# Expert token finding in rounds of two slot tiles, with one product per tile, and gathers spread over the scatter-adds

## What is computed

```python
probs = jax.nn.softmax(logits, axis=-1)
flat_probs = probs.transpose(2, 0, 1).reshape(En, T)
scores, tok_idx = jax.lax.top_k(flat_probs, cap)
xf = x.reshape(T, Dn)
toks = xf[tok_idx]
h = jax.nn.gelu(jnp.einsum('ecd,edh->ech', toks, w1) + b1[:, None, :])
y = jnp.einsum('ech,ehd->ecd', h, w2) + b2[:, None, :]
y = y * scores[..., None]
routed = jnp.zeros_like(xf).at[tok_idx.reshape(-1)].add(y.reshape(-1, Dn))
shared = jax.nn.gelu(xf @ sw1 + sb1) @ sw2 + sb2
out = (routed + shared).reshape(Bn, Sn, Dn)
```

## Time and profile before

| | us |
|---|---|
| median of three runs | 3782.42 (3778.78 to 3782.71) |
| the profiled execution's own time | 3778.83 |
| its span | 3777.0 |
| granted TensorE clock, mean over the span | 0.964 |
| tail phase, first product to the end of the span | 3120 to 3777 |

### The profile page before, as it was taken

One profiled execution on the slowest core, in us unless ns is written; L12 is line 12 of the kernel. 1 busy time (PEld: TensorE's weight loads), 2 busy tenths in 40 slices (PEclk: granted clock), 3 DMA queues, 4 the chain that ended last, 5 costly groups with the idle time before them and its releaser, 6 DMA issues. The chain is left out here.

```text
span 3777.0 us, 89362 instructions
## 1 busy us (share of the span) xinstructions
PE 3433.2 (91%) x30012; PEld 2631.4 (70%) x30012; DVE 2437.3 (65%) x6227; ACT 1999.1 (53%) x3884; POOL 2280.0 (60%) x2633
## 2 busy tenths in 40 slices
PE   7999999989999989999999999997997879879883
PEld 4577877777787767878777777774445666667763
DVE  2267776667777667777566777667986888653110
ACT  0156666656666656666665666674653433213331
POOL 0356663766665486666286666366985653464876
PEclk9999999999999999999999999998998999989887
DMA  6867664056766036666225667501111223232433
GB/s 221 259 117 130 129 128 81 19 100 125 130 128 128 8 75 129 129 126 133 46 40 108 129 128 130 95 2 36 33 28 38 64 60 45 54 85 44 71 59 31
DMA packets 456055, 342.06 MB, mean 91 GB/s; under 512 B 70659, under 2 KB 440171, under 8 KB 455595
## 3 DMA queue, kind: packets, MB, share of 16 engines
q1 hardware_dynamic: 404419, 275.69, 37.2%
q10 hardware_dynamic: 24224, 46.44, 3.7%
q0 software_dynamic: 27136, 16.42, 3.2%
HBM read 227.69 MB, written 109.29 MB: 89 GB/s over the span
## 5 line engine op out<-in xcount | busy, mean ns | idle before, releaser
L762 DVE TENSOR_REDUCE a_neg_max<-a_S 99x4 f32<-99x788 f32 x1024 | 1003.5, 980 | 473.6 <-PE a_S L337 470.3
L549 ACT ACTIVATE a_shared<-a_St 99x792 f32<-99x792 f32 (+1 forms) x1024 | 850.3, 830 | 631.7 <-PE a_St L354 620.1
L337 PE MATMUL a_S<-a_k_st,a_q_st 96*99 96x197 bf16 x4096 | 538.5, 254 | 40.1 <-DVE a_neg_max L762 40.1
L354 PE MATMUL a_St<-a_q_st,a_k_st 99*99 99x198 bf16 (+1 forms) x4096 | 529.0, 251 | 43.6 <-DMA a_q_st<-a_max_rows 27.0
L337 PEld LDWEIGHTS a_S<-a_k_st,a_q_st 96*99 96x99 bf16 x4096 | 389.7, 126 | 255.9 <-DVE a_neg_max L762 220.1
L373 PE MATMUL a_O<-a_shared,a_v_aug 99*32 99x198 f32 (+1 forms) x8192 | 466.8, 341 | 0.4
L354 PEld LDWEIGHTS a_St<-a_q_st,a_k_st 99*99 99x99 bf16 (+1 forms) x4096 | 391.1, 126 | 74.3 <-DMA a_q_st<-a_max_rows 34.4
L373 PEld LDWEIGHTS a_O<-a_shared,a_v_aug 99*32 99x32 f32 (+1 forms) x8192 | 247.7, 110 | 85.4 <-issue 2.6
L689 POOL CAST a_parts<-a_q_k 128x792 bf16<-128x792 f32 x128 | 107.8, 842 | 316.4 <-issue 270.1
L1822 POOL DMA_INDIRECT out<-h,token x128 | 209.6, 1638 | 103.9 <-DVE h L1872 47.4
L489 PEld LDWEIGHTS a_O<-a_w,a_shared 128*99 128x99 f32 x2048 | 242.7, 166 | 40.8 <-issue 23.2
(11 more groups left out here) (265 smaller groups left out, 7496.8 us busy)
## 6 DMA issues: line engine op xcount, KB each, us to landing
a_shared<-in_x ACTq DMA_DIRECT2D x64, 594.0 KB, 4.9
spill_q<-a_parts SPq DMA_DIRECT2D x384, 99.0 KB
spill_k<-a_parts SPq DMA_DIRECT2D x384, 99.0 KB
a_k_st<-spill_k SPq DMA_DIRECT2D x128, 297.0 KB
a_q_st<-spill_q SPq DMA_DIRECT2D x128, 297.0 KB
a_k_st<-spill_k SPq DMA_DIRECT2D x128, 198.0 KB
a_q_st<-spill_q SPq DMA_DIRECT2D x128, 198.0 KB
a_k_st<-spill_k SPq DMA_DIRECT2D x128, 99.0 KB
```

Of the source, the lines that this page charges most:

```text
L337: mm = nc.tensor.matmul(S[0:TC, j // 2, j % 2 * TB:j % 2 * TB + NTOK], q_st[p % 4][0:SPLIT, head, b * TB + c * TC:b * TB + (c + 1) * TC], ...
L354: mm = nc.tensor.matmul(St[0:keys, j // 2, j % 2 * TB:(j % 2 + 1) * TB], k_st[p][:, head, first:first + keys], q_st[p][:, head, b * TB:(b ...
L549: nc.scalar.activation(probs[0:keys, u % 4, :].rearrange("p (x t) -> p x t", x=2), St[0:keys, :, 0:2 * TB], ACT.Exp).then_inc(s["probs"], 1)
L762: nc.vector.tensor_reduce(out.rearrange("p (x y) -> p x y", x=2), S[0:TC, :, 0:2 * TB].rearrange("p x (y t) -> p x y t", y=2)[:, :, :, 0:N ...
```

## The change

- The two numbers per block lose their low part where it can go: the first token's number is stored as the number of the block (an integer up to 63) and multiplied by BLK on DVE. Three extra columns are left (RUN = BLK + 3): the first slot's high part, the block's number, the first slot's low part.
- A tile is found by one product of 232 columns. High and low part of the first slot are subtracted one after the other on DVE instead of being summed in PSUM.
- A round is two tiles and fills one bank; even rounds use C, odd ones X. `find` waits for the tokens of the round before the last.
- The four rounds of a turn stand, on PE, after half of `up(n + 1)`, after all of it, after half of `down(n)`, and after all of it. On DVE: rounds 0 and 1, one-hot, round 2, the sum, round 3.
- POOL gathers 13 experts ahead, and the other three in pairs of DMAs after the first twelve scatters.

```diff
-RUN = BLK + 4
+RUN = BLK + 3
-AHEAD = 12
+AHEAD = 13
...
                 def find(e, r, turned):
+                    n_r = 4 * e + r
                     if r == 0:
                         wait(pe, s["t_start"], 1)
                         wait(pe, s["hot"], 2 * (e + 1))
-                    wait(pe, s["token"], 4 * e + 2 * r)
+                    wait(pe, s["token"], n_r - 1)
                     wait(pe, s["copied"], turned)
-                    for k in range(4):
-                        at = r * WL + XCOLS[k]
-                        bank, to = (C, X)[k // 2], k % 2 * 256
-                        one = hot[e % 2][:, at:at + XL]
-                        nc.tensor.matmul(bank[0:XL, to:to + BLK], one, run64[:, e, 0:BLK], start=True, stop=True)
-                        for part in range(2):
-                            mm = nc.tensor.matmul(bank[0:XL, to + BLK:to + BLK + 2], one,
-                                                  run64[:, e, BLK + 2 * part:BLK + 2 * part + 2],
-                                                  start=(part == 0), stop=(part == 1))
+                    for t in range(2):
+                        at = r // 2 * WL + XCOLS[r % 2 * 2 + t]
+                        mm = nc.tensor.matmul((C, X)[r % 2][0:XL, t * 256:t * 256 + RUN], hot[e % 2][:, at:at + XL],
+                                              run64[:, e, :], start=True, stop=True)
                     mm.then_inc(s["found"], 1)
...
                     if n + 1 < PAIRS + UNITS:
-                        up(n + 1)
+                        up(n + 1, range(2))
+                    if e is not None:
+                        find(e, 0, turned)
+                        found += 1
+                    if n + 1 < PAIRS + UNITS:
+                        up(n + 1, range(2, 4))
...
                     if e is not None:
-                        find(e, 0, turned)
-                        found += 2
+                        find(e, 1, turned)
+                        found += 1
...
+                    if e is not None:
+                        find(e, 2, turned)
+                        found += 1
                     down(n, range(2, 4))
                     if e is not None:
-                        find(e, 1, turned)
-                        found += 2
+                        find(e, 3, turned)
+                        found += 1
...
                 for e in range(E):
                     scatter(e)
-                    if AHEAD + e // 2 < E:
-                        gather(AHEAD + e // 2, (0, 1) if e % 2 == 0 else (2, 3))
+                    if AHEAD + e // 4 < E:
+                        gather(AHEAD + e // 4, (e % 4,))
...
                 def tokens(e, r):
-                    n_r = 2 * e + r
-                    two = [bank[:].rearrange("p (t n) -> p t n", n=256) for bank in (C, X)]
+                    n_r, p = 4 * e + r, r % 2
+                    bank = (C, X)[p][0:XL, :].rearrange("p (t n) -> p t n", n=256)
+                    at = local[:, 2 * p:2 * p + 2]
                     dve.wait_ge(s["found"], n_r + 1)
-                    for k in range(2):
-                        nc.vector.tensor_tensor(local[:, 2 * k:2 * k + 2], slot[:, 4 * r + 2 * k:4 * r + 2 * k + 2],
-                                                two[k][0:XL, :, BLK], ALU.subtract).then_inc(s["local"], 1)
-                    for k in range(4):
-                        dve.wait_ge(s["local"], 2 * n_r + 1 + k // 2)
-                        nc.vector.tensor_scalar(junk[:, k, :], two[k // 2][0:XL, k % 2, 0:BLK], local[:, k:k + 1], None,
+                    nc.vector.tensor_tensor(at, slot[:, 2 * r:2 * r + 2], bank[:, :, BLK],
+                                            ALU.subtract).then_inc(s["local"], 1)
+                    dve.wait_ge(s["local"], 2 * n_r + 1)
+                    nc.vector.tensor_tensor(at, at, bank[:, :, BLK + 2], ALU.subtract).then_inc(s["local"], 1)
+                    dve.wait_ge(s["local"], 2 * n_r + 2)
+                    for t in range(2):
+                        k = 2 * p + t
+                        nc.vector.tensor_scalar(junk[:, k, :], bank[:, t, 0:BLK], local[:, k:k + 1], None,
                                                 ALU.is_le, ALU.add, accum_out=inside[:, k:k + 1]).then_inc(s["inside"], 1)
-                    for k in range(2):
-                        dve.wait_ge(s["inside"], 4 * n_r + 2 * k + 2)
-                        nc.vector.tensor_tensor(g.token[:, e, 4 * r + 2 * k:4 * r + 2 * k + 2], two[k][0:XL, :, BLK + 1],
-                                                inside[:, 2 * k:2 * k + 2], ALU.add).then_inc(s["token"], 1)
+                    dve.wait_ge(s["inside"], 2 * n_r + 2)
+                    nc.vector.scalar_tensor_tensor(g.token[:, e, 2 * r:2 * r + 2], bank[:, :, BLK + 1], float(BLK),
+                                                   inside[:, 2 * p:2 * p + 2], ALU.mult, ALU.add).then_inc(s["token"], 1)
...
                     if e is not None:
                         tokens(e, 0)
+                        tokens(e, 1)
                         if e + 1 < E:
                             one_hot(e + 1)
+                        tokens(e, 2)
                     total_of(n)
                     if e is not None:
-                        tokens(e, 1)
+                        tokens(e, 3)
```

More of the change, by code:

```diff
@@ L1519, in tail_phase @@
     with ExitStack() as ctx:
-        s = Sems(nc, ctx, "load_w load ew0 ew1 gel_pad eb2 bias b_part up gelu down sum0 sum1 sent0 sent1 "
+        s = Sems(nc, ctx, "load_w load ew0 ew1 gel_pad eb2 bias up gelu down sum0 sum1 sent0 sent1 "
                  "r_max r_sub r_exp r_sum r_inv r_prob r_turn r_copy scored table "
@@ L1548, in tail_phase @@
         cnt, n_gt, need, zero = sb("cnt", [128, 1]), sb("n_gt", [128, 1]), sb("need", [128, 1]), sb("zero", [128, 1])
-        before, base = sb("before", [128, 8]), sb("base", [128, 8])
+        before, block_no = sb("before", [128, 8]), sb("block_no", [128, 8])
         slot, order = sb("slot", [XL, 8]), sb("order", [B, SLOTS])
@@ L1595, in _ @@
                     sp.dma_start(dst[:], A[src]).then_inc(s["load_w"], 16)
-                for dst, src in ((same, "same_expert"), (sb2, "sb2"), (ahead, "ahead"), (base, "base"), (slot, "slot"),
+                for dst, src in ((same, "same_expert"), (sb2, "sb2"), (ahead, "ahead"), (block_no, "block_no"), (slot, "slot"),
                                  (order, "order"), (eb1, "eb1")):
@@ L2007, in _ @@
                         dve.wait_ge(s["load"], 112)
-                        nc.vector.tensor_copy(runx[:, :, BLK + 1], base[:]).then_inc(s["b_part"], 1)
-                        dve.wait_ge(s["b_part"], 1)
-                        nc.vector.tensor_tensor(runx[:, :, BLK + 3], base[:], runx[:, :, BLK + 1],
-                                                ALU.subtract).then_inc(s["t_final"], 1)
+                        nc.vector.tensor_copy(runx[:, :, BLK + 1], block_no[:]).then_inc(s["t_final"], 1)
                     if n == LAST_BIT + 1:
@@ L2035, in constants @@
         "order": np.repeat(np.arange(SLOTS, dtype=np.float32)[None], B, 0),
-        "base": ((p[:, None] // E * 8 + np.arange(8)[None, :]) * BLK).astype(np.float32),
+        "block_no": (p[:, None] // E * 8 + np.arange(8)[None, :]).astype(np.float32),
     }
```

## The result

| | before, us | after, us |
|---|---|---|
| median | 3782.57 (4 runs, 3778.78 to 3793.06) | 3751.65 (4 runs, 3745.78 to 3764.24) |
| ratio, 95% interval | | 0.9909 (0.9891 to 0.9928) |
| profiled execution | 3778.83, span 3777.0 | 3764.24, span 3762.5 |

By the two medians the kernel became 30.9 us faster; the ratio of 0.9909 would be 34. The profiled execution of after is the slowest of its four. Where the time went is read from three moments that every kernel of this study has: DVE's first one-hot operation (the finding stage begins), POOL's first scatter-add (it ends), and the first scatter-add of expert 15. They are starts of rows in the order of time, one profile of each kernel.

The account below looks back on a forecast made before the run. Finding turns were taken as limited by PE's late signals beside gathers, the scatter stage by POOL. Finding stage -27.4 and scatter stage -19.9 us took 3778.8 to 3731.5, as a median 3735; range 3711 to 3763.

Parts of the forecast that it names:

- rival 2: Finding stage: the hold stays at full price, turns lose only their own matmuls; -30.8 us, median 3752; 0.20 with rival 4.
- Scatter stage: Two gathers in twelve gaps: 18.15 us an expert, gain 19.9; signs: first scatters 18.0 to 18.4 apart, POOL standing under 0.6.
- Rival 4: Scatter stage: two gathers lengthen the landing, an expert takes 19.2 us, 15.8 missing from the forecast, 3751; 0.20 with rival 2.
- the hold: Finding stage: PE's signals reach others late, when a run of gathers is through; expected to remain but be ridden out.
- turns 17 to 27: Finding-stage turns beside gathers: fall from 12.82 us to POOL's gather pace of 10.8, -22.2 us in all.
- turn 16: Half its up pass moves behind the wait for the first one-hot: +1.6 us, less 0.7, so +0.9.
- turns 28 and 29: Two finding-stage turns taken as free of gathers: 9.2 us each for 10.50, -2.6 us.
- turns 30 and 31: The last two finding turns, which transpose tokens: 11.3 us each for 13.04, through a shorter token wait, -3.5 us.
- The thirteenth expert: Eight gathers move from scatter to finding stage, beside PE's work, and cost nothing by themselves.
- The turn without a hold: Finding-stage turn from PE's own work: 8.1 us at full clock, 9.2 at the granted clock of 0.88.
- rival 1: Finding stage: the hold goes, eleven turns at 9.2 us, stage gives 45.0, in all 64.9; median 3717; chance 0.30.
- Rival 3: Finding stage: each of four rounds meets the hold, a turn takes 16.2 us; slower, median 3794; chance 0.07.

Follow-up runs that it names:

- e7: The change with the gathers of the first thirteen experts as plain DMAs of fixed rows on SP's queue; 3720.62 us, single run.
- e12: e8 with each plain gather ahead cut into two of 60 rows, all issued by POOL; 3714.62 us, single run.
- e1: The changed kernel run again, unaltered; median 3757.06 us, ratio to before 0.9931.
- e8: The change with all gathers as plain DMAs of fixed rows, still issued by POOL; 3720.18 us, single run.
- the four corners: Finding stages of four kernels: before 207.0 us, the change 201.2, before with only the new gather order 210.6, the change with the old gather order 196.9.
- e7 to e12: e7, e8, e12, and the change with constant row numbers (3769.89 us), with waits for landed gathers (3765.99), with gathers ahead halved, rest by SP (3778.26).
- e5: The change with POOL's first gather waiting until the tokens of fourteen experts are found; 3835.85 us, single run.

## Why the prediction came out as it did

The time, 3751.65, lies in the range and 16.7 us above the forecast of 3735: of the 27.4 us forecast for the finding stage 5.8 came. It equals rival 2 (3752). The mechanism is rival 2's, but that the numbers meet within 1 us is luck, as shown below.

*Scatter stage: right.* Forecast -19.9 us, 273.5 from expert 0 to 15; measured 274.6, -18.8. An expert takes 18.30 us for 18.15, and the 1.2 us for slower first ones didn't come; the two errors partly cancel. The longest distance of 18.8 and the 0.8 us of standing lie just outside the signs that were named (18.4 and 0.6). The shortest wait in rows 3 is 2.60 us, not the 2.67 that was taken. The rest is that up to 0.8 us of standing time remain where two gathers don't quite fill the wait for the landing. Rival 4, with 19.2 an expert, is excluded in every run: over all of them an expert takes 18.3 to 18.5 us on average with two gathers a gap (single ones up to 19.7, in e7). The Trainium skill's rule ("DMA: Bandwidth & Descriptors", section "Anatomy of one DMA — SWDGE (gpsimd) path") of about 2.0 us fixed is met by the plain gathers of 60 rows in e12, from issue to landing:

```profile
DMA to landing us min/median/max: 1.8/2.1/7.2
```

For scatter-adds it doesn't hold: POOL still waited 2.70 us after the last issue had ended at 3735.62.

*Finding stage: the step that failed is "the hold ... to be ridden out, so that turns 17 to 27 run at POOL's pace of 10.8 us".* Measured between DVE's sums of the shared turns:

| term | forecast, us | measured, us |
|---|---|---|
| turn 16 | +0.9 | 13.5 for 10.2, +3.3 |
| turns 17 to 27 | 11 x (10.8 - 12.82) = -22.2 | 12.53 for 12.82, -3.2 |
| turns 28 and 29 | -2.6 | 22.1 for 21.0, +1.1 |
| turns 30 and 31 | -3.5 | 21.1 for 26.0, -5.0 |
| the stage from end to end | -27.4 | -5.8 |

(The four measured terms add up to -3.8; the other 1.9 lie before the first and behind the last sum.) Beside gathers a turn takes nearly what it took: 0.3 us less in after, 0.7 in e1. POOL still stood idle for 22.2 us between its gathers (24.1 before), so it did not become the bound, and the split of the rounds couldn't help: what is late isn't the tokens but any signal of PE, those of the up and down passes too.

Two terms were also sized wrongly for reasons of their own. *Turns 28 and 29* were taken as free of gathers, at 10.50 each. But POOL issued until 3412.6 in before and until 3429.1 in after. Turn 28 lies beside gathers in both (11.2 and 13.2 us), and only turn 29 is at most partly so (9.8 and 8.9). *Turn 16* takes 14.8 to 14.9 us in e7, e8 and e12 too, so its loss isn't the hold. In e8 the half of the up pass that moved behind the wait for the first one-hot takes 3.42 us; the forecast had 1.6.

```profile
3263.01 3.42 PE L1648 MATMUL z_U<-xT,z_sw 128*128 128x458 f32 x4
```

```profile
3263.00:3266.40 3.40, 3.40 (x6) 1.21 (x5) 1.31 (x7) 0.64 (x1) 1.11 (x2) 0.50 0.19 52
```

PE had stood 3.81 us just before, and the granted clock of the stretch is 0.50, the lower of its two levels (1.2 GHz); a half pass at the full clock takes 1.80 us.

*The thirteenth expert: the second step that failed.* It was costed at nothing because POOL's issues lie beside PE's work. But PE pays for each expert's gathers beside it: 3.6 to 4.3 us by the four corners. Without them the new finds give 9.4 to 10.1 us, where rival 2's finding term was -10.9. This is why rival 2's sum is near: its term for the finds is about right, its missing cost of the thirteenth expert is 4 us and its scatter term 1 us too good, and the median came out some 6 us lower than the stages do. With e1's 22.4 us in place of 30.9 the sum of -30.8 would have been 8 us off.

*The turn without a hold.* I had 9.2 us from 8.1 at a clock of 0.88; e7, e8 and e12 show 8.7. The clock was not 0.88 there but 0.98 to 1.00, and the turn 0.6 longer than 8.1. So rival 1 (hold gone, 3717) was near in its price: 3714.62 to 3720.62 measured. Its finding stage was 6 us too long (162 for 156), its scatter stage 4 too short (273.5 for 277 to 278).

*DVE's round* is 3365.32 + 0.16 - 3364.07 = 1.41 us where I took 1.31 as the upper bound. At 8.7 us a turn DVE was busy 120 of 157 us and still did not set the pace.

*Turns 30 and 31* take 10.4 and 10.7 us in after, and the same in the three runs without a hold; 11.3 was forecast, 13.0 was before. That part of the change works as meant.

*Rival 3* (each round meets the hold, slower than before) fell: turns stayed at 12.5.

What stays open is how an indirect gather holds PE. That it isn't the rows, their number, the freshness of the row numbers, the landing, or a full queue is shown by e7 to e12, each alone. The indirect scatter-adds don't do the same to PE, nor do runs of two or four gathers between them; why a longer run does is open.

## What to carry to other kernels

A gap that the issuing engine spends waiting for its own landing can be filled to the size of the gap and no further: two gathers fit into 2.7 us, four cost 2.3 us too much, and the sum from rows came out to 1 us over fifteen experts. Before shortening the work beside an unnamed wait, find what the wait belongs to by swapping one form of the suspected transfer for another with the same bytes. Here four rounds were rearranged around a hold that goes with 45 us of the stage and stays as long as long runs of indirect gathers lie beside PE's work. Where spans drift by 10 us ahead of the change, measure the stages between fixed moments of the program.

## What the runs showed of the hardware

- Long runs of indirect gathers issued by POOL delay PE's signals and its next products; plain gathers issued by POOL don't, even without a break, and indirect scatter-adds with two or four gathers between them don't either (0 of 936 signals over 0.3 us late). In after single signals came up to 9.7 us late, in e5, with 104 gathers in a row, 79 us; in e7, e8 and e12 0.1 us at most.
- An indirect gather of 120 rows takes POOL 0.99 us and one of 60 rows 0.93, each with 0.30 ahead of it. A plain one takes 0.53 of 120 rows and 0.52 of 60, with nothing ahead.
- The mean granted clock of the finding stage, between the two levels of 1.2 and 2.4 GHz, was 0.88 in after, where PE stood 28 of 157 us, and 0.98 to 1.00 in e7, e8 and e12, where it stood 3 to 4. Part of the 45 us of the hold may be this; the two weren't separated.
